# A decoder layer on one core: VectorE's mask steps moved behind the first queries and keys

## What is computed

```python
x = layernorm(x + self_attention(x))          # 16 heads of 16; two score terms mixed by a gate; causal
x = layernorm(x + cross_attention(x, ctx, mask))
x = layernorm(x + ffn(x))                     # 704 wide, inputs and weights quantized to FP4 in blocks of 16
```

```python
scores = where(mask == 0, -1e9, q @ k.T / sqrt(16)); attn = softmax(scores)
```

## Time and profile before

| what | value |
|---|---|
| median of three timed executions | 622.29 us |
| the profiled execution | 618.94 us, of which the span is 617.2 us |
| TensorE matmul busy | 549.6 us, 89% |
| VectorE busy | 512.0 us, 83% |
| ScalarE busy | 285.8 us, 46% |
| GpSimd busy | 177.5 us, 29% |

### The profile page before, as it was taken

The page is one execution under the profiler, slowest core; times in us unless marked ns, Lnnn a source line. Parts: engine busy times, 40 slices in busy tenths (PEclk is TensorE's granted clock), DMA queues, the critical chain, the costliest instruction groups (busy, mean ns, idle before and its releaser), DMA issues.

```text
span 617.2 us, 16429 instructions
## 1 busy us (share of the span) xinstructions
PE 549.6 (89%) x5724; PEld 351.0 (57%) x5724; DVE 512.0 (83%) x1444; ACT 285.8 (46%) x671; POOL 177.5 (29%) x251
## 2 busy tenths in 40 slices
PE   3686898889999999999999998998999998899875
PEld 2554354546565666666576656564665765455543
DVE  3587888787889989898999997567989996887894
ACT  1342145466454555545545455454455554444412
POOL 7014141423132414233242413141232424211211
PEclk9998699899999999999999998798999999998999
DMA  8366553445453554536263636345452635330000
GB/s 253 80 187 186 157 154 110 146 124 139 138 147 95 128 165 110 168 102 186 72 180 106 170 90 179 107 124 157 112 170 77 171 102 153 88 89 16 26 8 26
DMA packets 75933, 77.14 MB, mean 125 GB/s; under 512 B 13068, under 2 KB 67404, under 8 KB 75852
## 3 DMA queue, kind: packets, MB, share of 16 engines
q1 hardware_dynamic: 73612, 73.75, 42.1%
q10 hardware_dynamic: 2240, 2.35, 1.3%
HBM read 39.89 MB, written 27.00 MB: 108 GB/s over the span
## 4 chain that ended last, share of the span: by engine, by line
PE 50%; DVE 29%; issue 9%; ACT 4%; DMA 4%; SPq 2%; POOL 2%; DVEq 0%; POOLq 0%; ACTq 0%
PE misc L2248 16%; PE misc L2234 7%; DVE junk L1431 4%; PE prob L2173 4%; PE score L2164 3%; PE xpv L2223 3%; PE prob L2179 3%; PE apv L2211 3%; PE misc L2289 3%; DVE amax L1423 2%; DVE xden L1470 2%; DVE qt L1348 2%; PE misc L2276 2%; DVE qt L1338 2%; PE score L2140 2%
## 5 line engine op out<-in xcount | busy, mean ns | idle before, releaser
L1431 DVE CUSTOM_DVE_ANT_0 junk<-score,maskbias 112x375 bf16<-112x375 f32 x256 | 128.8, 541 | 27.3 <-PE score L2164 26.4
L932 ACT ACTIVATE xP<-prob 128x448 f32<-128x448 f32 (+1 forms) x192 | 94.0, 541 | 54.4 <-PE prob L2179 53.9
L2248 PE MATMUL misc<-wguT,xqT 128*128 128x352 f32 x224 | 80.8, 489 | 1.9 <-ACT xqT L892 1.1
L741 POOL TENSOR_TENSOR move_a<-mT,eye 128x448 bf16<-128x448 bf16 x32 | 36.3, 1152 | 73.6 <-ACT mT L892 73.6
L2164 PE MATMUL score<-xK,xQ 64*128 64x375 f16 x256 | 52.0, 339 | 5.8 <-DVE xmax L1431 2.6
L765 POOL TENSOR_TENSOR rstd<-veps,half 128x1 f32<-128x1 f32 (+1 forms) x44 | 28.2, 640 | 96.7 <-DVE veps L1506 96.7
L761 POOL TENSOR_TENSOR aattT<-anum,aden 128x224 f32<-128x224 f32 x16 | 11.1, 693 | 155.0 <-DVE aden L1470 107.9
L2248 PEld LDWEIGHTS misc<-wguT,xqT 128*128 128x128 f32 x224 | 39.4, 193 | 25.8 <-issue 9.0
L741 POOL TENSOR_TENSOR move_x<-mT,eye 128x448 bf16<-128x448 bf16 x32 | 33.1, 1040 | 72.0 <-ACT mT L892 72.0
L2223 PE MATMUL xpv<-xP,xV 128*32 128x112 f32 (+1 forms) x1536 | 51.5, 268 | 0.5 <-ACT xP L932 0.3
L2248 PE MATMUL misc<-xwvT_s,ctxT_s 128*128 128x256 f32 (+1 forms) x192 | 49.9, 392 | 1.5 <-ACT kcf L892 1.1
(11 more groups left out here) (158 smaller groups left out, 1095.5 us busy)
## 6 DMA issues: line engine op xcount, KB each, us to landing
xk_dram<-xk_parts SPq DMA_DIRECT2D x64, 192.0 KB, 3.2
xK<-xk_dram SPq DMA_DIRECT2D x16, 768.0 KB, 4.6
ctxT_s<-in_ctxT SPq DMA_DIRECT2D x15, 375.0 KB, 3.7
aq_dram<-aq_parts SPq DMA_DIRECT2D x64, 64.0 KB, 2.5
ak_dram<-ak_parts SPq DMA_DIRECT2D x64, 64.0 KB, 2.4
aQ<-aq_dram SPq DMA_DIRECT2D x16, 256.0 KB, 2.9
aK<-ak_dram SPq DMA_DIRECT2D x16, 256.0 KB, 2.9
xq_dram<-xq_parts SPq DMA_DIRECT2D x64, 64.0 KB, 2.1
```

Source lines behind the costliest of these rows:

```text
L741: pool.tensor_tensor(dst[:, big], mT[:, n, big].rearrange("p (j q) -> p j q", j=2).unsqueeze(2).to_broadcast([P, 2, GH, HS]), eye[:].unsqu ...
L932: act.activation(xP[0:KEYS[c], g % 2, c], prob[m][0:KEYS[c], 0:GH * S].rearrange("p (h q) -> p h q", h=GH), ACT.Exp).then_inc(probs.taken[ ...
L1431: dve.tensor_tensor_reduce(junk[:, m], score[m][0:S, 0:SC], maskbias[:], 1.0, -3.0e38, ALU.add, ALU.max, xmax[:, b.par, h // (2 * GH), h / ...
L2248: mm = pe.matmul(misc[m][0:rows_, 0:cols], actT(c), weightT(c), start=(c == 0), stop=(c == DT - 1))
```

## The change

`masks` is split in two. `mask_rows` holds the wait for the transfers, `maskbias` and `alive`; `mask_columns` holds `shift_x`. The signal `mask_ready` moves from the step that makes `alive` to the last memset of `shift_x`. In VectorE's ramp `masks` stood in front of `mixed_bias`; `mask_rows` now stands behind the first `k_lo`, and `mask_columns` three quantization steps later, in front of the `k_lo` of batch 1. No other engine's program changes.

```diff
-            def masks():
+            def mask_rows():
                 dve.wait_ge(w_mask, 48)
                 dve.nop(nofuse=True)
                 step(dve.tensor_scalar(maskbias[:], mask_i, 0, NEG, ALU.is_equal, ALU.mult))
+                step(dve.tensor_scalar(junk[:, 0], mask_i, 0, None, ALU.not_equal))
+                step(dve.tensor_reduce(alive[:], junk[:, 0], AX.X, ALU.max))
+
+            def mask_columns():
                 step(dve.memset(shift_x[:], 0.0))
                 step(dve.tensor_scalar(shift_x[:, :, 0:SC], mask_t_i.rearrange("p (j s) -> p j s", j=2), 0, NEG, ALU.is_equal, ALU.mult))
-                for a in range(2):
-                    step(dve.memset(shift_x[HALF * a:HALF * a + GH], 1.0))
-
-                step(dve.tensor_scalar(junk[:, 0], mask_i, 0, None, ALU.not_equal))
-                dve.tensor_reduce(alive[:], junk[:, 0], AX.X, ALU.max).then_inc(mask_ready, 1)
+                step(dve.memset(shift_x[0:GH], 1.0))
+                dve.memset(shift_x[HALF:HALF + GH], 1.0).then_inc(mask_ready, 1)
...
             def ramp():
-                masks()
                 mixed_bias()
                 q_lo(at[-2], at[0])
                 k_lo(at[-2], at[0])
+                mask_rows()
                 quant_weight(0, 0)
                 quant_weight(0, 1)
                 quant_weight(0, 2)
+                mask_columns()
                 k_lo(at[-1], at[1])
                 q_lo(at[-1], at[1])
                 quant_weight(0, 3)
```

## The result

The changed kernel took 619.05 us in the median of 17 executions, the kernel before 620.93 in 17 beside them. The ratio is 0.9943 with a 95% interval of 0.9915 to 0.9970: faster by 0.57%, 3.5 us. The ratio leaves out five executions of the changed kernel as disturbed, because they lie over 1.5% above its fastest (610.97), and none of the kernel before, which flatters the change; over all 17 against 17 the means are 618.45 and 620.76, 2.3 us apart. With the executions of the experiments it is 29 against 154, means 617.61 and 620.74: **3.1 us faster, with an uncertainty of 1.1**. I had forecast 0.8.

A forecast was written before the change was run, and what follows sets the result against it. No single bound: the chain lies on TensorE for half the span and VectorE for 29%, with the ramp late by its mask. About 2.25 us early, 0.8 kept: 622.29 - 0.8 = 621.5 us, range 619.4 to 623.3.

The forecast's parts named there:

- What goes early: Ramp: with the mask steps behind it, the bias copy runs at about 16.40; first queries and ctx_k start 2.2 to 2.25 us earlier.
- Where a part of it goes back: VectorE behind the first keys: the moved mask steps make it late at the second keys, leaving a 0.83 us shift.
- the mark: Start of quant_weight(0, 3) on VectorE in the ramp, forecast at 28.42 against 29.25 us before.
- What follows it: After the ramp: VectorE's instructions follow on each other, ctx_v of the second batch at 32.2; shift everywhere 0.8 us.
- Nothing later in the kernel is tied to an absolute time: Rest of the kernel: the initial loads have landed, so the 0.8 us shift holds everywhere.
- SyncE's second put: SyncE's second put of queries, at 29.61 before, is issued 0.9 to 1.0 us early, and so is all behind it.
- The rival of the clock: Closing TensorE's hole at 18 to 20 opens one at 25.9 to 28.0; lower clock, 624 to 625 us; chance 0.08.
- The sum: Whole kernel: profiled 618.94 becomes 618.1; timed median 622.29 less 0.8 gives 621.5 us.
- I carry the difference over: Timed median 622.29 lies 3.4 us above the profiled execution; that difference is kept in the forecast time.
- the clock 0.08 to the good: Rival: the low-clock stretch of 64 to 74 us shrinks, giving 618 to 619 us; chance 0.08.
- The range: Whole kernel, 8 in 10: 619.4 to 623.3 us, taking in the whole gain and no gain with scatter 0.7 to 1.
- a full gain of 2.2 us: Rival: the whole 2.2 us from the ramp stays, giving 620.1 us; chance 0.13.

The follow-up runs named there:

- third: Changed kernel with the column part of the mask steps done twice in a row at its place; 3.1 us over the changed kernel (uncertainty 1.8).
- eleventh: Changed kernel with the column part of the mask steps done three times in a row; 5.9 us over the changed kernel (uncertainty 2.0).
- second experiment: Against the kernel before, only mask_rows moved behind the first k_lo, mask_columns in front of mixed_bias; 2.0 us under the kernel before (uncertainty 2.4).
- fourth: Against the kernel before, mask_rows stays in front of mixed_bias, mask_columns goes far behind, ahead of the first cross queries; 2.7 us under it (uncertainty 1.9).
- tenth: Changed kernel with nine filler matmuls in front of TensorE's work; 2.3 us under the kernel before (uncertainty 1.9), 0.9 over the changed kernel.
- twelfth: Against the kernel before, mask_rows between mixed_bias and the first queries' low parts, mask_columns far behind; mean 617.36, 3.4 us under it (uncertainty 2.4).
- fifth experiment: Kernel before with ten more filler matmuls between the first queries and ctx_k; 1.7 us slower (uncertainty 1.8), with its repeat 0.7 over (1.1).
- eighth: The kernel before, unchanged, against itself; mean 622.28, 1.7 us over its other executions (uncertainty 1.5), ratio 1.0061.

## Why the prediction was wrong

- *What goes early* was right in kind and 0.2 us too small: ScalarE's first queries came at 17.69, not 17.90, because the bias and the mixed weight on TensorE were 0.23 earlier in that profile.
- *Where a part of it goes back* was right: no wait is left between the column part and the second keys, VectorE decides there, and of the 2.46 us by which the first keys' low parts came early, 1.27 are left at the mark (forecast: 0.83 of 2.25). TensorE's hole in front of the third keys is 1.87. The terms were 0.23 us too large in all: the row part 0.11, the column part 0.14 and the second keys 0.03, less 0.05 that the three quantization steps took more.
- *What follows it* was right as far as a profile can tell: the third keys were freed by the second keys' low parts, `ctx_v` came at 31.77 (32.2 forecast), and the added work of the third and eleventh experiments is carried one for one. "Nothing later in the kernel is tied to an absolute time" holds for these, but not for every change: the loads of instructions come at their own places and met a transfer in four of the experiments. (The 0.9 to 1.0 us given there for SyncE's second put don't follow: 29.34 less 28.5 is 0.8. Nothing hangs on it.)
- *The rival of the clock* is where it failed. The step was: "Against it: the old hole of 2.2 us was of the same length and cost no clock." I read one execution's hole as the kernel's hole, and even a hole of that length isn't safe (2.29 us in the second experiment, with the clock at 0.50 behind it). In the order of before, the hole lies between two things that aren't tied to each other: it begins when TensorE has done the first queries, which moves by 1.5 us with the rise of the clock (16.56 to 18.10), and it ends when the mask has landed and 4.5 us of steps are done. In two of five profiles it was 3.5 and 3.8 us, and there the clock fell and the ramp was 1.8 and 4.6 us late. The change doesn't just move such a loss to another place: the new hole is there because TensorE waits for VectorE, and a fall of the clock behind it cost 0.2 us between the two marks in both profiles of the changed kernel (23.87 and 23.86 us in place of 23.67).
- *The sum* failed with it: "I carry the difference over" took a profile with a lucky ramp for the mean of the kernel. Over the five profiles the change is worth 2.8 us in place of 1.27. The start of the sum was off besides: 622.29 is the median of three executions, that of 17 is 620.93. So of the 2.45 us between the forecast 621.5 and the measured 619.05, 1.37 are the start and the rest is the gain. The direction of the rival was also wrong. I gave the clock 0.08 to the good, and that was the case that came about, in another place than I had named for it.
- The range ended 0.35 us above the measured median. Its lower end held a full gain of 2.2 us and 0.7 of scatter, taken from the start that was 1.4 too high; from 620.93 the same range would have held the result, though the gain in it was still far too small.

What stays open: how often the clock rises early in the kernel before, and with it how the 3.1 us divide; what would be gained by filling the hole if no load of instructions met the transfer; why the second experiment, with a second mark of 54.81 in its one profile, was 2.0 us under the kernel before (uncertainty 2.4); and whether marks under 27 are worth anything at the end. The fourth, tenth and twelfth experiments, with marks of 26.0 to 26.3, were 0.4 over, 0.9 over and 0.3 under the changed kernel, each with an uncertainty of 2 or more.

## What to carry to other kernels

A hole of TensorE between two chains that aren't tied to each other (here its own work and a transfer with steps behind it) has a length that differs from execution to execution; look at several profiles before you call it harmless, and at what waits for TensorE behind it. Moving work away from in front of such a hole, to a place where the engine that does it decides, took away both here: time, and the risk of the clock. Where executions scatter by 3 us, find the shift in an early mark of several profiles, and check with added work that such a shift reaches the end. Take a second mark further on too: the first one alone hid the 1.5 us that the filler lost again.

## What the runs showed of the hardware

- The level of TensorE's clock in the first 16 us is one thing in one execution and another in the next, for identical code: three matmuls of 448 columns from about 13.1 us on took 0.73 to 1.33 us, the eight of 128x128 in f32 behind them 1.05 to 1.81. The granted clock in the view by stretches reads 1.00 for all of them.
- An early rise can cost: with filler matmuls from 6 us on, the kernel before became 4.4 us slower. The work that was done sooner left a hole of 4.2 us in front of `ctx_k`, with the clock at 0.50 behind it (2.8 us at the first mark), and further on a transfer landed 1.1 us late.
- A load of instructions (one packet of 0.02 MB) and a transfer of the kernel can meet. `aden<-aoT` landed after 1.9 us in the fourteen profiles without such a packet in it, and after 2.6 to 3.1 us in the four with one. With ten more matmuls early in TensorE's program that packet came at 44.5 us in place of 50.5 (the fifth experiment against the eighth).
- The same `maskbias` step (112x375, int32 to bf16) took 0.34 to 0.36 us with GpSimd idle. In the ten profiles in which it began while GpSimd's memset of `xV` (2.67 us) was under way, it took 0.46 to 1.11 us and ended 0.20 to 0.21 us behind that memset each time. The 0.57 us of the earlier trace rows are such a case, and this is why the forecast of that step was 0.22 too large.
